# The first batch of a 32-batch attention kernel on Trainium2: where the weight scales are found, how Wo is split and turned, and in which order the first jobs run

## The chip, the cores and the metric

The kernel runs on one core of one Trainium2 chip. Its time is the device time of the whole program in microseconds. Three runs of the kernel before took 1008.40, 1008.94 and 1008.09 us; the median, 1008.4 us, is what the change is measured against.

## The reference

For 32 batches of 256 rows by 512 columns, one layer of graph attention with 16 heads of 32 columns, and a residual. The adjacency matrix is added to the logits (twice, as spatial and as edge encoding).

```python
h = jnp.maximum(_layernorm(x, axis=-1), 0.0)
q = split_heads(h @ Wq.T); k = split_heads(h @ Wk.T); v = split_heads(h @ Wv.T)
a = jnp.einsum('bhnd,bhmd->bhnm', q, k) * D ** (-0.5) + (adj + adj)[:, None]
row_nonzero = jnp.any(a != 0, axis=-1, keepdims=True)
a = jnp.where(row_nonzero, a, -jnp.inf)
p = jax.nn.softmax(a, axis=-1)            # nan -> 0
o = jnp.einsum('bhnm,bhmd->bhnd', p, v).transpose(0, 2, 1, 3).reshape(B, N, D)
x = x + o @ Wo.T
```

x is (32, 256, 512), adj (32, 256, 256) and each weight (512, 512), all in f32.

## The kernel before

**Arithmetic.** Products are made of f16 halves: every operand is split into a rounded part (`_hi`) and the rest (`_lo`), and three products (hi·hi, hi·lo, lo·hi) are summed in PSUM. ScalarE (ACT) writes the rounded part, VectorE (DVE) or GpSimd (POOL) the rest. A weight is brought to a known size first: DVE takes the largest magnitude of each partition (`weight_max`, L610), TensorE (PE) turns the column of 128 maxima into a row (`turn_max`, L881), DVE takes the row's maximum (L616), PE spreads it over the partitions (`spread_max`, L887), and DVE makes the scale by five or more small instructions (`weight_scale`, L622 to L638). PE turns each weight by 16 transposes of 128x128 (`turn_weights`, L873), and ACT and DVE read the turned weight from PSUM and write `w_hi` (L481) and `w_lo` (L650), in four chunks of 128x512.

**Slots.** The program is written out as 34 slots of 16 steps each. Slot number b + 1 works on head 0 to 15 of batch b and prepares batch b + 1: jobs q01, q23, k01, k23, v0, v1 (24 matmuls for a q or k job, 12 for a v job, L978, run in two halves at steps 2j and 2j + 1), and the output jobs o0 and o1 of batch b - 1. In the first slot there are no heads; it makes the weights and batch 0's q, k and v. The second slot has heads but no output jobs. Each engine executes its own list in order, and semaphores tie the lists together. Scores of a group of four heads (L996) are made at steps 12, 0, 4 and 8; `logits` (L690, DVE) follow in the three steps after, then `probs` (L509, exp on ACT with the row sum), the f16 rounding `p` (L522, ACT), the rest of it (L411, POOL), and a transpose by DMA issued from SP (L345). Products with v (`values`, L1046) run at step 12 for heads 0 to 7 and at step 4 of the next slot for heads 8 to 15.

**Around the change.** The first slot has a table of its own (`job_at`, `turn_h_steps`, `v_steps`): jobs 0 to 3 in steps 0 to 7, jobs v0 and v1 in steps 12 to 15, and the second batch's h is turned at steps 9 and 12. The maxima of Wv and Wo are taken at steps 3 and 4 of the first slot on DVE. Wo is turned by PE in the second slot, one chunk of four transposes at each of steps 11 to 14 (`turn_last_weights`, L899), through the two banks that the jobs use (PJ_BANK), and job q01 of the third slot waits until three or four of its chunks have been taken. A store that held a weight is used again later: `pt` for heads 8 to 15 lies in Wq's and Wk's store, `norm_t` in Wv's.

## Time and profile before

| what | us |
|---|---|
| median of three runs | 1008.4 |
| the profiled execution, its own time | 1011.0 |
| its span, first to last instruction | 1009.2 |
| PE busy | 967.0 (96%) |
| ACT busy | 926.8 (92%) |
| DVE busy | 853.0 (85%) |
| POOL busy | 861.7 (85%) |
| first head's exp starts | 48.0 |

The time of the execution is 1.8 us above its span. Shares over the whole span say little of the opening: in the first 48 us no head's softmax runs, and from about 84 us on each slot repeats the one before it. The rows below therefore are of the first 100 us by their starts, with a few of the repeating part to compare.

### The profile page before, as it was taken

What the parts mean: (1) busy time and instruction counts of PE and PEld (TensorE: products, weight loads), DVE (VectorE), ACT (ScalarE), POOL (GpSimd) and SP (SyncE); (2) the same over time, 40 slices, a digit from 0 to 9 for tenths busy, and PEclk for the clock granted to TensorE, in tenths of its full rate; (3) what the DMA queues carried; (4) which work ended last, traced back from release to release, by engine and by line L of the source; (5) the groups of instructions that cost most, each with busy time, mean ns of one, the idle gap of its engine ahead of it and who ended that gap; (6) DMA issues with size and microseconds to landing.
All of it is one profiled execution on the core that took longest, in us unless ns stands there. A gap on an engine that the chain in (4) does not pass through costs nothing.

```text
span 1009.2 us, 33752 instructions
## 1 busy us (share of the span) xinstructions
PE 967.0 (96%) x11596; PEld 666.3 (66%) x11596; DVE 853.0 (85%) x3090; ACT 926.8 (92%) x3025; POOL 861.7 (85%) x936
## 2 busy tenths in 40 slices
PE   6788999999999999999999999999999999999965
PEld 5566766676776667677666777666677766667632
DVE  6778988889898888989888898988889898888863
ACT  3399999999999999999999999999999999999992
POOL 1178989899988989998898999989899988989894
PEclk9899999999999999999999999999999999999988
DMA  6088999999999999999999999999999999999995
GB/s 250 11 145 144 190 188 188 183 193 200 179 190 189 189 188 192 187 199 184 185 182 194 188 201 187 185 194 175 193 192 195 177 196 183 190 188 176 172 178 117
DMA packets 569579, 182.59 MB, mean 181 GB/s; under 512 B 542784, under 2 KB 550976, under 8 KB 569408
## 3 DMA queue, kind: packets, MB, share of 16 engines
q1 hardware_dynamic: 569408, 180.43, 98.1%
q8 instruction: 93, 1.52, 0.6%
q14 instruction: 78, 0.64, 0.2%
HBM read 29.36 MB, written 16.78 MB: 46 GB/s over the span
## 4 chain that ended last, share of the span: by engine, by line
PE 58%; DVE 27%; issue 8%; ACT 5%; POOL 2%; DMA 1%; DVEq 0%; POOLq 0%; ACTq 0%; SPq 0%
PE ps L978 36%; DVE logits L690 14%; PE ps L1046 8%; PE ps L996 7%; DVE stats L595 4%; PE ps L861 3%; ACT probs L509 3%; DVE q_lo L753 2%; DVE o_norm L720 2%; PE ps L1022 1%; DVE some L708 1%; DVE w_max L610 1%; ACT p L522 1%; PE ps L950 1%; POOL p L411 1%
## 5 line engine op out<-in xcount | busy, mean ns | idle before, releaser
L411 POOL TENSOR_TENSOR p<-probs,p 128x512 f16<-128x512 f32 x512 | 586.5, 1162 | 95.8 <-ACT p L522 95.6
L509 ACT ACTIVATE probs<-logits,row_min 128x256 f32<-128x256 f32 x1024 | 514.3, 513 | 1.3 <-DVE row_min L690 1.3
L690 DVE CUSTOM_DVE_ANT_0 logits<-ps,adj_s,sigma 128x256 f32<-128x256 f32 x1024 | 438.0, 475 | 9.8 <-PE ps L996 9.7
L522 ACT ACTIVATE p<-probs 128x512 f16<-128x512 f32 x512 | 324.2, 633 | 0.0
L978 PE MATMUL ps<-ht_hi,w_hi 128*128 128x256 f16 x1024 | 280.9, 274 | 6.4 <-DVE w_lo L650 1.9
L978 PE MATMUL ps<-ht_lo,w_hi 128*128 128x256 f16 x1024 | 280.2, 274 | 0.0
L978 PE MATMUL ps<-ht_hi,w_lo 128*128 128x256 f16 x1024 | 280.1, 274 | 0.0
L509 ACT ACTIVATION_READ_ACCUMULATOR probs<-logits,row_min 128x1 f32 x1024 | 211.4, 206 | 0.0
L978 PEld LDWEIGHTS ps<-ht_hi,w_hi 128*128 128x128 f16 x1024 | 100.4, 98 | 34.3 <-DVE q_lo L753 11.4
L978 PEld LDWEIGHTS ps<-ht_lo,w_hi 128*128 128x128 f16 x1024 | 100.6, 98 | 14.5
L978 PEld LDWEIGHTS ps<-ht_hi,w_lo 128*128 128x128 f16 x1024 | 100.6, 98 | 12.0
L978 PE MATMUL ps<-w_hi,o_hi 128*128 128x512 f16 x248 | 94.7, 382 | 3.6 <-POOL o_lo L437 3.6
L978 PE MATMUL ps<-w_hi,ht_hi 128*128 128x512 f16 x256 | 98.1, 383 | 0.0
L978 PE MATMUL ps<-w_lo,ht_hi 128*128 128x512 f16 x256 | 97.6, 381 | 0.0
L978 PE MATMUL ps<-w_hi,ht_lo 128*128 128x512 f16 x256 | 97.5, 381 | 0.0
L753 DVE SCALAR_TENSOR_TENSOR k_lo<-ps,k_hi 128x512 f16<-128x512 f32 x64 | 43.7, 683 | 63.3 <-ACT k_hi L539 63.3
L978 PE MATMUL ps<-w_hi,o_lo 128*128 128x512 f16 x248 | 94.5, 381 | 0.0
L978 PE MATMUL ps<-w_lo,o_hi 128*128 128x512 f16 x248 | 94.4, 381 | 0.0
L690 DVE DVE_READ_ACCUMULATOR2_ANT row_min<- 128x1 f32 x1024 | 81.4, 80 | 0.0
L422 POOL TENSOR_TENSOR norm<-recip,some 128x256 f32<-128x256 f32 x128 | 78.8, 615 | 1.1 <-PE ps L1022 1.1
L437 POOL TENSOR_TENSOR o_lo<-o_norm,o_hi 128x512 f16<-128x512 f32 x64 | 74.3, 1160 | 5.3
L743 DVE SCALAR_TENSOR_TENSOR v_lo<-ps,v_hi 128x512 f16<-128x512 f32 x64 | 44.2, 691 | 40.3 <-ACT v_hi L549 37.8
(88 smaller groups left out, 1654.9 us busy)
## 6 DMA issues: line engine op xcount, KB each, us to landing
xs<-in_x SPq DMA_DIRECT2D x32, 512.0 KB, 4.5
out<-xs SPq DMA_DIRECT2D x64, 256.0 KB, 2.9
adj_raw<-in_adj SPq DMA_DIRECT2D x32, 256.0 KB, 3.6
pt<-p SPq DMA_TRANSPOSE x256, 4.1
w_nat<-p SPq DMA_TRANSPOSE x256, 3.3
w_nat<-in_L_gnn_Wq SPq DMA_DIRECT2D x1, 1024.0 KB, 6.3
w_nat<-in_L_gnn_Wk SPq DMA_DIRECT2D x1, 1024.0 KB, 9.1
w_nat<-in_L_gnn_Wv SPq DMA_DIRECT2D x1, 1024.0 KB, 11.2
```

What stands on the lines that cost most here:

```text
L411: g.tensor_tensor(p16[:, c % 2, k, 1], probs[:, h % 4].rearrange("p u n -> p (u n)"), p16[:, c % 2, k, 0], ALU.subtract).then_inc(p_split, 1)
L422: g.tensor_tensor(norm[:, c % 2].rearrange("p u (j d) -> p u j d", j=HC), recip[:].unsqueeze(3).broadcast_to(wide), some[:].unsqueeze(3).b ...
L437: g.tensor_tensor(o_lo[:, t.par(d), both, :], o_norm[:], o_hi[:, t.par(d), both, :], ALU.subtract).then_inc(o_split, 1)
L509: e = a.activation(probs[:, h % 4, u, :], logits[:, h % 4, u, :], ACT.Exp, bias=row_min[:, t.par(d), u, h:h + 1], scale=-1.0, accum_out=ro ...
L522: a.activation(p16[:, c % 2, k, 0], probs[:, h % 4].rearrange("p u n -> p (u n)"), ACT.Copy)\
L595: v.bn_stats(stats[:, u, :], xs[:, t.batch(d) % X_RING, u, :]).then_inc(stat_step, 1)
L690: v.tensor_tensor_reduce(out=logits[:, h % 4, u, :], in0=ps[:, S_BANK + h % HC, N * u:N * u + N], in1=adj_s[:, t.par(d), u, :], scale=sigm ...
L743: v.scalar_tensor_tensor(out=v_lo[:, t.par(d), u, :], in0=ps[:, PJ_BANK + u, :], scalar=DOWN, in1=v_hi[:, t.par(d), u, :], op0=ALU.mult, o ...
L753: v.scalar_tensor_tensor(out=lo[:, t.par(1), 2 * g:2 * g + 2, :].rearrange("p c n -> p (c n)"), in0=ps[:, PJ_BANK + g, :], scalar=-DOWN if ...
L978: m = mm(o, l, r, start=start, stop=stop)
L996: m = mm(ps[:, S_BANK + j, N * u:N * u + N], Q[x][HD * j:HD * j + HD, t.par(d), c, P * u:P * u + P], K[y][HD * j:HD * j + HD, t.par(d), c, ...
L1046: m = mm(o, (v_hi, v_lo)[a][:, t.par(d), mh, HD * h:HD * h + HD], pt(c, j)[:, 2 * NU * b + mh:2 * NU * b + mh + NU + 1:NU, :], start=(mh = ...
```

## The change

All edits concern the first two slots, and how Wo lies in SBUF.

1. **Scales from row sums.** For Wk, Wv and Wo, ACT computes the sum of magnitudes of each row of 512 (`sum_weight`, Abs with an accumulated sum, four instructions for a weight), and DVE takes the largest of the four sums of a partition. The scale constants follow (SUM_DOWN, SUM_UP). Wq keeps its true maximum.
2. **Wq in halves.** Its load is two DMAs, and its maximum two DVE instructions of 1024 columns, joined by a third small one.
3. **Second x ahead of Wv** in SP's list of loads.
4. **First slot's order.** Wk is turned and scaled after job q01 instead of before it; the first job of a weight starts chunk by chunk as `w_lo` comes; v0 runs at steps 8 and 9, the first scores at step 12, v1 at steps 13 and 14. Batch 0's second h chunk goes through a bank of its own. The row test of batch 0 moves to the second slot.
5. **Wo.** It is split as it lies (`round_wo` on ACT, `split_wo` on DVE, one row block at each of steps 8 to 11 of the second slot) and turned by four DMA transposes issued from SP at steps 12 to 15; PE's 16 transposes and the wait of job q01 are gone. The output jobs read it as `wo16[:, :, 4*b + c, :]`, four pieces of 128 columns, where they read 512 columns in a row.

```diff
-            load_w(0, wq_d)
+            sp.dma_start(w_nat[:, 0, 0:2], wq_rows[:, 0:2]).then_inc(w_in[0], 16)
+            sp.dma_start(w_nat[:, 0, 2:4], wq_rows[:, 2:4]).then_inc(w_second_half_in, 16)
             load_w(1, wk_d)
+            sp.dma_start(xs[:, 1], xv[1]).then_inc(x_in[1], 16)
             load_w(2, wv_d)
-            sp.dma_start(xs[:, 1], xv[1]).then_inc(x_in[1], 16)
...
-        WO_STEP = 11
+        WO_STEP = 8
+        FIRST_STEPS = [(0, 1), (2, 3), (4, 5), (6, 7), (8, 9), (13, 14)]
...
+                    if t is second and s >= 12:
+                        sp.wait_ge(wo_split, s - 11)
+                        sp.dma_start_transpose(wo16[:, s - 12], w16[:, 2, s - 12]).then_inc(wo16_in, 16)
...
+            def sum_weight(w, o):
+                act.wait_ge(w_in[w], 16)
+                spare = {1: w_nat[:, 0, o, :], 2: probs[:, o].rearrange("p u n -> p (u n)"), 3: w_nat[:, 2, o, :]}[w]
+                a.activation(spare, w_nat[:, w, o, :], ACT.Abs, accum_out=w_sum[:, w - 1, o:o + 1])\
+                 .then_inc(w_summed, 1)
+            def round_wo(o):
+                act.wait_ge(scales_ready, 4)
+                a.activation(w16[:, 2, o, 0:D], w_nat[:, 3, o, :], ACT.Copy, scale=w_scale[:, 3:4])\
+                 .then_inc(wo_hi, 1)
...
-            def weight_max(w):
-                dve.wait_ge(w_in[w], 16)
-                v.tensor_reduce(out=w_max[:, w:w + 1], in_=w_nat[:, w].rearrange("p o k -> p (o k)"),
-                                axis=AX.X, op=ALU.max, apply_absolute_value=True).then_inc(w_max_found, 1)
+            def weight_sum_max(w):
+                dve.wait_ge(w_summed, NC * w)
+                v.reduce_max(w_max[:, w:w + 1], w_sum[:, w - 1, :], AX.X).then_inc(w_max_found, 1)
+            def split_wo(o):
+                dve.wait_ge(wo_hi, o + 1)
+                v.scalar_tensor_tensor(out=w16[:, 2, o, D:2 * D], in0=w_nat[:, 3, o, :], scalar=w_scale[:, 3:4],
+                                       in1=w16[:, 2, o, 0:D], op0=ALU.mult, op1=ALU.subtract).then_inc(wo_split, 1)
...
             turn_weights(0, (0, 1))
             turn_max(0)
-            turn_h(first, 1, 0)
+            turn_h(0, 0)
             spread_max(0)
+            turn_h(0, 1, PJ_BANK + 1)
             turn_weights(0, (2, 3))
-            turn_h(first, 1, 1)
-            turn_max(1)
-            spread_max(1)
-            turn_weights(1)
...
-                                    W[b][:, 3, c, :], i == 0, i == len(steps) - 1))
+                                    wo16[:, :, NC * b + c, :], i == 0, i == len(steps) - 1))
...
-                    if t.batch(1) == 2 and j in (0, 1):
-                        pe.wait_ge(wt_taken, NC * 3 + NC - 1 + j)
+                    if j == 6 and t.batch(-1) == 0:
+                        pe.wait_ge(wo16_in, 16 * NC)
...
+                for i in range(half * part, half * part + half):
+                    o, l, r, start, stop = products[i]
+                    if t.first and j in (0, 2, 4) and i < 12 and i % 3 == 0:
+                        pe.wait_ge(wt_taken, NC * (j // 2) + i // 3 + 1)
                     m = mm(o, l, r, start=start, stop=stop)
```

**ACT, first slot.** Before, from the first rounding of h (`ht_hi`) to the first exp (`probs<-logits`):

```order
L486 ACTIVATE ht_hi<-ps 128x512
L481 ACTIVATE w_hi<-ps,w_scale 128x512 x4
...
L532 ACTIVATE q_hi<-ps 128x512 x2
L539 ACTIVATE k_hi,k_sum<-ps 128x256 x4
...
L486 ACTIVATE ht_hi<-ps 128x512 x2
L549 ACTIVATE v_hi<-ps 128x512
L509 ACTIVATE probs,row_sum<-logits,row_min 128x256 x4
```

In the changed kernel the same stretch (the rows of L514 are the sums of magnitudes, of Wk, Wv and twice half of Wo):

```order
L507 ACTIVATE w_hi<-ps,w_scale 128x512 x4
L514 ACTIVATE w_nat,w_sum<-w_nat 128x512 x4
L570 ACTIVATE q_hi<-ps 128x512
L514 ACTIVATE probs,w_sum<-w_nat 128x512 x4
...
L577 ACTIVATE k_hi,k_sum<-ps 128x256 x2
L514 ACTIVATE w_nat,w_sum<-w_nat 128x512 x2
L587 ACTIVATE v_hi<-ps 128x512
L525 ACTIVATE ht_hi<-ps 128x512
...
L547 ACTIVATE probs,row_sum<-logits,row_min 128x256 x2
```

Twelve sums came in between the roundings, which are spread out: a weight's `w_hi` now stands behind the q or k job that precedes it.

**DVE, first slot.** Before, from Wq's `w_lo` to Wv's scale:

```order
L650 SCALAR_TENSOR_TENSOR w_lo<-ps,w_scale,w_hi 128x512 x4
...
L631 TENSOR_SCALAR sigma<-w_pow 128x1
...
L753 SCALAR_TENSOR_TENSOR q_lo<-ps,q_hi 128x512
L610 TENSOR_REDUCE w_max<-w_nat 128x1 x2
...
L616 TENSOR_REDUCE w_row_max<-ps 1x1
L753 SCALAR_TENSOR_TENSOR k_lo<-ps,k_hi 128x512
...
L690 ISA logits,row_min<-ps,adj_s,sigma 128x256
```

After, from the same `w_lo` to the first logits:

```order
L716 SCALAR_TENSOR_TENSOR w_lo<-ps,w_scale,w_hi 128x512 x4
L649 BN_STATS stats<-xs 128x6 x2
L674 TENSOR_REDUCE w_max<-w_sum 128x1
L815 SCALAR_TENSOR_TENSOR q_lo<-ps,q_hi 128x512
...
L700 TENSOR_SCALAR sigma<-w_pow 128x1
...
L815 SCALAR_TENSOR_TENSOR k_lo<-ps,k_hi 128x512
L724 SCALAR_TENSOR_TENSOR ht_lo<-ps,ht_hi 128x512
L805 SCALAR_TENSOR_TENSOR v_lo<-ps,v_hi 128x512
L752 ISA logits,row_min<-ps,adj_s,sigma 128x256
```

The long reductions over a whole weight are gone from DVE's list after Wq's, and the first logits stand ahead of v1's rest.

**SP, end of the second slot.** Before, the transposes of heads 8 to 15 (into `w_nat`) stand in a row, ahead of the third adjacency load:

```order
L345 DMA_TRANSPOSE w_nat<-p 128x8x128 x8
L355 DMA adj_raw<-in_adj 128x2x256
L345 DMA_TRANSPOSE pt<-p 128x8x128 x6
```

After, Wo's four are put between the last five of them:

```order
L360 DMA_TRANSPOSE w_nat<-p 128x8x128 x4
L369 DMA_TRANSPOSE wo<-w_nat 128x8x128
L360 DMA_TRANSPOSE w_nat<-p 128x8x128
...
L374 DMA adj_raw<-in_adj 128x2x256
L360 DMA_TRANSPOSE pt<-p 128x8x128 x6
```

The middle two rows stand four times in turn; each transpose is of the same size as a head's.

## Rows read from the trace of the kernel before

**Rows 1.** The page's first part: busy time of TensorE over the span

```profile
PE 967.0 (96%) x11596; PEld 666.3 (66%) x11596; DVE 853.0 (85%) x3090; ACT 926.8 (92%) x3025; POOL 861.7 (85%) x936
```

**Rows 2.** Stretches: length; busy us (instructions) per engine; granted clock; DMA share; GB/s

```profile
80.00:84.00 4.00, 3.59 (x36) 2.32 (x36) 3.34 (x12) 4.00 (x13) 3.92 (x5) 0.57 0.37 71
...
150.00:180.00 30.00, 29.88 (x388) 20.81 (x380) 26.36 (x97) 29.11 (x97) 27.38 (x31) 1.00 1.06 193
```

**Rows 3.** Timeline of SP, adjacency loads of two slots 26 apart: start, us

```profile
144.24 0.53 SPq L355 DMA_DIRECT2D adj_raw<-in_adj  x1
...
911.41 0.53 SPq L355 DMA_DIRECT2D adj_raw<-in_adj  x1
```

**Rows 4.** The chain of waits of the first 120 us: start, us, what

```profile
25.43 4.38 DVE w_max L610 x2
...
41.85 2.56 PE ps L978 x6
```

**Rows 5.** Timeline of DVE, first two slots: start, us, instruction, idle before

```profile
7.58 2.29 DVE L610 TENSOR_REDUCE w_max<-w_nat 128x1 f32<-128x2048 f32 x1 [1.00 <-DMA w_nat<-in_L_gnn_Wq]
...
15.91 2.70 DVE L650 SCALAR_TENSOR_TENSOR w_lo<-ps,w_scale,w_hi 128x512 f16<-128x512 f32 x4
...
45.86 0.48 DVE L690 CUSTOM_DVE_ANT_0 logits<-ps,adj_s,sigma 128x256 f32<-128x256 f32 x1 [2.65 <-PE ps L996]
...
80.72 0.48 DVE L690 CUSTOM_DVE_ANT_0 logits<-ps,adj_s,sigma 128x256 f32<-128x256 f32 x1
```

**Rows 6.** Timeline of ACT, first slot and start of the second

```profile
12.48 2.42 ACT L481 ACTIVATE w_hi<-ps,w_scale 128x512 f16<-128x512 f32 x4 [0.69 <-DVE w_scale L638]
...
47.98 0.50 ACT L509 ACTIVATE probs<-logits,row_min 128x256 f32<-128x256 f32 x1
...
53.44 0.62 ACT L522 ACTIVATE p<-probs 128x512 f16<-128x512 f32 x1
53.96 0.58 ACT L532 ACTIVATE q_hi<-ps 128x512 f16<-128x512 f32 x1
```

**Rows 7.** Timeline of PE, first slot

```profile
7.70 1.94 PE L873 MATMUL ps<-ident,w_nat 128*128 128x128 f32 x8 [7.70 <-DMA w_nat<-in_L_gnn_Wq]
...
20.23 0.42 PE L978 MATMUL ps<-ht_hi,w_hi 128*128 128x256 f16 x1
...
22.36 0.29 PE L978 MATMUL ps<-ht_lo,w_hi 128*128 128x256 f16 x1
...
29.04 0.27 PE L978 MATMUL ps<-ht_hi,w_lo 128*128 128x256 f16 x1
30.47 0.28 PE L978 MATMUL ps<-ht_hi,w_hi 128*128 128x256 f16 x1 [1.16 <-DVE q_lo L753]
...
33.61 1.97 PE L873 MATMUL ps<-ident,w_nat 128*128 128x128 f32 x16
```

**Rows 8.** DMA issues of the first 60 us: KB each, median us from issue to landing

```profile
w_nat<-in_L_gnn_Wv SPq DMA_DIRECT2D x1, 1024.0 KB, 11.2
```

**Rows 9.** Timeline of PE, end of the second slot

```profile
75.63 0.66 PE L899 MATMUL ps<-ident,w_nat 128*128 128x128 f32 x4 [1.33 <-DVE v_lo L743]
...
80.41 0.37 PE L978 MATMUL ps<-ht_hi,w_hi 128*128 128x256 f16 x1 [1.91 <-DVE w_lo L650]
...
90.72 0.42 PE L1046 MATMUL ps<-w_nat,v_hi 128*32 128x256 f16 x8
```

**Rows 10.** Timeline of ACT, waits in the second slot's end and the third

```profile
76.32 0.69 ACT L481 ACTIVATE w_hi<-ps,w_scale 128x512 f16<-128x512 f32 x1 [0.63 <-PE ps L899]
...
94.17 0.38 ACT L539 ACTIVATE k_hi<-ps 128x256 f16<-128x256 f32 x1 [0.71 <-PE ps L978]
```

**Rows 11.** The page's costliest groups: an output job's matmul, busy us, mean ns

```profile
L978 PE MATMUL ps<-w_hi,o_hi 128*128 128x512 f16 x248 | 94.7, 382 | 3.6 <-POOL o_lo L437 3.6
```

**Rows 12.** Transposes on SP in 68 to 84 us: ns min/median/max; landing

```profile
L345 SPq DMA_TRANSPOSE w_nat<-p x8: 1232/1312/2222, 68.2 to 82.7; - x8
...
DMA to landing us min/median/max: 3.0/3.2/4.4
```

More of the change, by code:

```diff
@@ L85, in emit @@
         w_nat = sb("w_nat", [P, 4, NC, D])
-        w_hi = sb("w_hi", [P, 4, NC, D], F16)
-        w_lo = sb("w_lo", [P, 4, NC, D], F16)
+        w_hi = sb("w_hi", [P, 3, NC, D], F16)
+        w_lo = sb("w_lo", [P, 3, NC, D], F16)
+        wo16 = sb("wo16", [P, NC, 2 * NC, P], F16)
+        w_half = sb("w_half", [P, 2])
+        w_sum = sb("w_sum", [P, 3, NC])
         w16 = w_nat.bitcast(F16)
@@ L453, in slot @@
                     split_probs(t, s)
+                    if t.first:
+                        continue
                     if s == 3 and later(t, 2):
@@ L557, in slot @@
                 for s in range(H):
-                    if s == 0 and t is second:
-                        take_v(t, 0, 1)
-                    if s in v_steps(t) and t.nxt:
-                        take_v(t, 1, v_steps(t).index(s))
-                    if t.nxt:
+                    if t.nxt and not t.first:
                         if s in (2, 4):
@@ L797, in slot @@
                         take_o(t, 0, 0)
-                    if later(t, 2) and s == 10 and not t.first:
-                        take_h(t, 2, 1, 2 * t.batch(2) + 2)
+                    if s == 10 and not t.first:
+                        for k in h_rests(t, s):
+                            take_h(t.batch(2), k)
                     for b, u in residuals(t, s):
                         residual(b, u)
-                    if s == 1 and t is second:
-                        take_v(t, 0, 1)
-                    if s - 1 in v_steps(t) and t.nxt:
-                        take_v(t, 1, v_steps(t).index(s - 1))
@@ L808, in slot @@
+                    if t is second:
+                        if s == 0:
+                            take_v(t, 0, 1)
+                            weight_row_max(3)
+                        if s == 2:
+                            weight_scale(3)
+                            test_rows(first)
+                        if s - WO_STEP in range(NC):
+                            split_wo(s - WO_STEP)
                     if s % 4 == 3 and t.cur:
@@ L953, in project_last, with project @@
                         m.then_inc(pj_full, full_step(tail, 6 + u))
[L955 to L959 removed]
+            def project(t, j, part):
                 if part == 0:
@@ L1077, in slot @@
                         turn_probs(t, 0, s // 4 - 1)
-                    if later(t, 2) and s in turn_h_steps(t):
-                        turn_h(t, 2, turn_h_steps(t).index(s))
-                    project(t, s)
+                    for k in h_turns(t, s):
+                        turn_h(t.batch(2), k)
+                    for j, half in halves(t, s):
+                        if t.uses(j):
+                            project(t, j, half)
                     if s == 3 and t.prev:
@@ L1091, in slot @@
                         values(t, 0, 0)
-                    if t.nxt and s == 13:
+                    if t.nxt and s == 13 and not t.first:
                         row_test(t)
-                    if t is second and s in range(WO_STEP, WO_STEP + NC):
-                        turn_last_weights(s - WO_STEP)
+                    if t is second and s == 1:
+                        row_test(first)
                     if t is tail and s in (0, 1, 5, 6):
```

268 lines of the change are left out of this document (158 added, 110 removed).

## The prediction

> **What bounds the kernel now.** I read the shares first, then stretches of the repeating part, then the opening as a chain of waits and as a timeline of each engine. Over the span TensorE (PE) is busy 96% of the time [rows 1], and in the repeating part 29.88 of 30 us, ScalarE (ACT) 29.11, VectorE (DVE) 26.36 [rows 2]. A slot there takes (911.41 - 144.24) / 26 = 29.5 us [rows 3]. PE is the bound, ACT has some 0.9 us a slot to spare, and the change takes nothing from a repeating slot. So it can only move the start of that part: each microsecond by which PE's work stands earlier at the third slot comes off the end, as long as nothing behind it is late.
>
> The opening is bound otherwise. The first exp starts at 47.98 [rows 6], behind the first logits at 45.86 [rows 5]. On the way the chain shows DVE with two whole-weight maxima, 4.38 us, with a job's remainder queued behind them, and job v0 near the slot's end, six matmuls of 512 columns in 2.56 us [rows 4], 0.43 each, which is the lower clock. From the first exp to 94 us ACT is nearly full. The third slot's first matmul comes at 80.41, after PE stood 1.91 us for Wo's remainder, and 1.33 us ahead of Wo's second chunk [rows 9]; ACT itself waits 0.63 us for that chunk and 0.71 us for job k01 [rows 10].
>
> **Prices from the rows.** A whole-weight maximum 2.29 us on DVE, half of it 1.15; `w_lo` 2.70 / 4 = 0.675 a chunk [rows 5]. `w_hi` 2.42 / 4 = 0.605; a 128x512 pass from SBUF 0.52 (`p` at 53.44, the next at 53.96); two exps of 256 columns, with their sums, 0.49 apart [rows 6]. A matmul of 256 columns starts every (22.36 - 20.23) / 10 = 0.213 us at first and every (29.04 - 22.36) / 61 = 0.11 us then: 12 take 2.6 or 1.3 us. That is TensorE's level of 1.2 GHz and then the one of 2.4. A 128x128 transpose is 0.22 to 0.24 us at the lower and 0.11 to 0.12 at the higher (8 in 1.94, 16 in 1.97) [rows 7]. Not in the trace is a sum of magnitudes over 512 columns: between 0.52 (without a sum) and 0.98 (two of 256 with one). I take 0.62, near the first, since two instructions are started and two sums read in the 0.98; 12 of them are 7.4 us of ACT, 6.2 to 11.8 at the ends.
>
> **First slot, step by step** (times on the clock of before, us). Wq's second half lands where Wq did, 7.58; the first half's maximum is by then done, so the whole is known at about 9.05 instead of 9.87. PE's list lets 0.5 of that through: eight transposes first (7.70 to 9.64) [rows 7]. Wq's scale comes at 11.9, `w_hi` would start 0.5 earlier but both h chunks now go first: `w_hi` from 12.5 to 14.9, as before [rows 6]. DVE: two h remainders to 13.25, four `w_lo` to 15.95. Job q01 starts with the first chunk at 13.95, not at 20.23: Wk's maximum, scale and turning are no longer ahead of it. It follows the chunks to 16.6 and ends at about 18.4 (17.9 to 19.2 with the clock). ACT sums Wk meanwhile, 14.9 to 17.4. Then Wk is turned (18.4 to 20.6), its scale is ready at 21.9; q23's halves run at 20.7 and 22.3, `w_lo` of Wk comes 23.3 to 25.55 on DVE, k01 runs 24.5 to 27.2, Wv is turned to 29.0, k23 ends at 31.6, v0 at 34.2. Wv landed 11.2 us after an issue in the first 3 us [rows 8], so before 14.2, and lands some 1.4 later behind the second x (512 KB); it is summed from 19.15, so that swap costs nothing. A slower sum (0.98) would delay Wk's maximum by 1.5 us, which q01's second half mostly hides, and Wv's by as much, before it delays k01: about 1 us in all.
>
> After v0: h remainder and v remainder on DVE (35.5 to 36.65), then the first logits at 36.65, against 45.86: 9.2 earlier. The second slot must also take Wo's scale, on DVE between logits (about 1.2 us there), and v1 ends at 39.2. Its q01 waits for the turn of Wo's maximum, which DVE makes behind its logits (40.7), then for nothing: 41.0 to 44.5 with a group of scores inside, the row test to 44.9, then ACT's `q_hi`, which stood at 53.96 [rows 6]. So the second slot runs **9.0** us earlier.
>
> **Second slot's end.** Splitting Wo costs ACT and DVE four passes each, as before; ACT's are 0.52 instead of 0.605 less overlap, 0.2 us in all. Gone are ACT's waits of 0.63 and 0.71 [rows 10] and, I estimate, 0.4 us in ones under 0.2: 9.0 + 0.2 + 1.7 = 10.9 by ACT's list. PE loses 16 transposes and their waits, and starts the third slot when its products with v are done, at some 74.5 of the old clock; but after half a job it must stop for the next batch's first logits, whose last stood at 80.72 to 81.2 [rows 5]. That wait of 5 us is longer than the three before 80.41, after which the matmuls ran at 0.21 apart and the stretch's clock was 0.57 [rows 2, 9]; so I let the lower clock last as long as it did there, about 3.3 us, until 83.7. Before, 80.41 to 85.5 held half a job (12 x 0.213 = 2.6), the scores and the other half (12 x 0.11 = 1.3). After, the first half lies in the wait; the scores begin at 81.2 + 0.3 for the hand-over - 0.8 for the waits that ACT no longer has = 80.7, take 1.3 at the lower clock, and the second half ends at about 84.3: 1.2 sooner. PE: 9.0 + 1.2 = 10.2, less than ACT's 10.9, and from there PE is full as before. **10.2** off; 11.5 if PE stays at the higher clock there.
>
> The four DMA transposes stand in SP's list between those of heads 11 to 15. A transpose holds SP 1.31 us, and lands 3.2 us after its issue [rows 12]. Heads come each 1.5 to 2 us, with a second transpose between two heads SP needs 2.6: the last head's is some 2.7 us late. Products with v need it at 90.72 before [rows 9]; it was issued at 82.7 and landed near 86, a slack of over 4, of which the earlier PE takes 1.2. It just holds: I put 0 in the sum, 2 at the upper end. On a transpose's price the Trainium skill says (DMA: Bandwidth & Descriptors, Latency and other measured facts) that the effective rate is 261 GB/s; for 256 KB that would be an estimate of 1.0 us, so SP's own 1.31 would be what limits, as I have it.
>
> **The sum.** The profiled execution took 1011.0, its span and 1.8 around it. Minus 10.2 it is 1000.8. The median stands 2.6 under that execution, so 1008.4 - 10.2 = **998.2**.
>
> **The rivals.**
> *PE falls to the lower clock at the second slot's head.* In the changed order PE stands 1.5 us between v1 (39.2) and Wo's maximum (40.7), after another 0.75 us. For: after waits of 1.33 and 1.91 us with little between, the 256-column matmuls from 80.41 on took 0.21 each, and the clock granted was 0.57 [rows 2, 9]. Against: a wait of 1.16 us at 29.3 left the pace at 0.11 [rows 7]. Then q01 is 2.6 us longer and the scores 0.6, in front of ACT's `q_hi`: 3 us, of the 10.2 remain 7, time 1001.2. The same price has a first slot that stays at the lower clock until k01 (two halves of 1.3). The Trainium skill (TensorE: Matmul & The Clock Gate, What's actually happening) has it that the throttled state is the default and that activity releases it; by that rule the gaps between chunk-wise matmuls at 14 to 16.6 speak for this rival, and the trace's 10 slow matmuls from 20.23 agree.
> *Wo's transposes are late.* If a transpose takes 2.2 us, the maximum seen [rows 12], the last head's lands 4 x 0.9 = 3.6 us later still, and PE waits about 2 at its values: 1000.2, or 1001 with slower sums.
> *Slower than before: the output jobs read Wo in four pieces.* 24 matmuls a slot in 31 slots, 744 in all, change their moving operand. It decides from 10.2 / 744 = 14 ns each. Against it: products with v read two pieces of 128 columns, and eight of them, four at a time, last 0.42 from start to end at 90.72, no longer than a single whole-row one of 0.27 and one pace of 0.11 more [rows 9, 7]. If four pieces cost 20 ns where two cost none, the time is 998.2 + 14.9 = 1013.
> *The opening's gain does not reach the end* (ACT, DVE or POOL keeps the second slot where it was, or the gain is used up): 1007 to 1010. The small waits of rows 10 and PE's 29.88 of 30 speak against it.
>
> **Chances.** Forecast 0.50 (996.7 to 999.7); clock 0.20 (1000 to 1003); late transposes and slow sums 0.12 (1000 to 1002); more gain than summed, 11.5 or above because PE keeps the higher clock, 0.10 (995 to 997); no gain 0.04; slower 0.04. The range goes from 995.2 to 1002.6. A measurement of this kernel tells 0.2%, 2.0 us, from no change: faster 0.92, same 0.04, slower 0.04.
>
> **What would show it.** Right: first logits at about 36.7, first `p` near 41, q01 from 14 us, in the second slot's end one long wait of PE, for logits, with the third slot's first half job ahead of it, and from the third slot on the same rows as before, 10 us earlier, 29.5 apart. Sums of 0.62 on ACT. Wrong: matmuls 0.21 us apart after 40 us, a wait of values for a transpose in the third slot, or a mean above 382 ns for an output job's matmul [rows 11]. A time above 1004 would mean that a slot's own length changed or that ACT's list in the first slot is the bound.

## The result, and the profile after

The changed kernel took 1005.13 us (median of 5 runs, 1003.96 to 1005.36), the kernel before 1008.94 (5 runs, 1008.09 to 1012.47). The ratio on record is 0.9941 with a 95% interval of 0.9923 to 0.9959, so 5.9 us gained, between 4.1 and 7.8. The two medians alone lie 3.8 us apart: three of the five runs of the kernel before are those behind the prediction's 1008.4, the two others took 1009.77 and 1012.47. A second measurement of both kernels, the first experiment below, gives 5.2 us. Forecast were 998.2 and a gain of 10.2; the time lies 2.5 us above the top of the range. It is faster, by little more than half of what was forecast. That the time lies outside the range is in part a matter of the base: the measured ratio applied to 1008.4 would be 1002.5, just inside. The gain is what missed.

The span of the profiled execution is 1003.4 us, where it was 1009.2. Busy time by the page of the changed kernel, to be read beside [rows 1]:

```profile
PE 959.6 (96%) x11580; PEld 660.2 (66%) x11580; DVE 850.0 (85%) x3092; ACT 934.5 (93%) x3049; POOL 862.3 (86%) x936
```

ACT has 7.7 us more work (twelve sums of 0.61 to 0.65), PE 16 matmuls less, as the change says.

**The repeating part.** The adjacency loads of the changed kernel in SP's timeline, the same two as in [rows 3]:

```profile
138.25 0.53 SPq L374 DMA_DIRECT2D adj_raw<-in_adj  x1
...
905.33 0.53 SPq L374 DMA_DIRECT2D adj_raw<-in_adj  x1
```

They come 5.99 and 6.08 us sooner, and 767.08 apart where it was 767.17. A slot's length is unchanged: all that is gained or missed is decided before 138 us. Twenty-six slots further nothing has been given back.

**First slot.** DVE's timeline of the changed kernel (start, us, instruction, idle before), to be read beside [rows 5]:

```profile
7.86 1.22 DVE L665 TENSOR_REDUCE w_half<-w_nat 128x1 f32<-128x1024 f32 x1 [0.36 <-DMA w_nat<-in_L_gnn_Wq]
...
17.94 0.16 DVE L674 TENSOR_REDUCE w_max<-w_sum 128x1 f32<-128x4 f32 x1 [0.17 <-ACT w_nat L514]
...
37.03 0.48 DVE L752 CUSTOM_DVE_ANT_0 logits<-ps,adj_s,sigma 128x256 f32<-128x256 f32 x1
```

ACT's, beside [rows 6]:

```profile
15.33 0.65 ACT L514 ACTIVATE w_nat<-w_nat 128x512 f32<-128x512 f32 x1
...
41.39 0.62 ACT L560 ACTIVATE p<-probs 128x512 f16<-128x512 f32 x1
...
45.00 0.60 ACT L570 ACTIVATE q_hi<-ps 128x512 f16<-128x512 f32 x1
```

A maximum that took DVE 2.3 us is one of 0.16 over four sums. The first logits come 8.83 us sooner than before (36.65 was forecast, 37.03 came), and `q_hi` of the second slot at 45.00 instead of 53.96: 8.96 us, where the forecast had 9.0. Part of this is the spread between executions: in the six traces of the experiments that leave the first slot as it is here, the first logits stand at 36.14 to 36.66.

**Second slot.** Here the gain is lost. PE's timeline of the changed kernel, its two longest waits between 60 and 85 us:

```profile
67.98 0.40 PE L1063 MATMUL ps<-k_hi,q_hi 32*128 32x256 f16 x4 [3.60 <-DVE row_min L752]
...
76.20 0.29 PE L1063 MATMUL ps<-k_hi,q_hi 32*128 32x256 f16 x4 [1.69 <-DVE row_min L752]
```

These are scores, the first at step 12 of the second slot. The scores' matmuls overwrite a bank that DVE's last logits of the group before must have read, so they wait for `row_min`. The first group is now 4.04 us earlier than before, no longer 8.96. In the kernel before it began here:

```profile
72.02 0.29 PE L996 MATMUL ps<-k_hi,q_hi 32*128 32x256 f16 x4 [0.38 <-DVE row_min L690]
```

DVE's list of the changed kernel just ahead of it (L679 is `split_wo`):

```profile
58.45 1.28 DVE L679 SCALAR_TENSOR_TENSOR w_nat<-w_nat,w_scale 128x512 f16<-128x512 f32 x1 [2.42 <-ACT w_nat L520]
59.66 0.68 DVE L815 SCALAR_TENSOR_TENSOR k_lo<-ps,k_hi 128x512 f16<-128x512 f32 x1
...
61.04 0.75 DVE L679 SCALAR_TENSOR_TENSOR w_nat<-w_nat,w_scale 128x512 f16<-128x512 f32 x1 [0.71 <-ACT w_nat L520]
...
63.64 0.75 DVE L679 SCALAR_TENSOR_TENSOR w_nat<-w_nat,w_scale 128x512 f16<-128x512 f32 x1
...
66.12 0.76 DVE L679 SCALAR_TENSOR_TENSOR w_nat<-w_nat,w_scale 128x512 f16<-128x512 f32 x1
...
67.36 0.47 DVE L752 CUSTOM_DVE_ANT_0 logits<-ps,adj_s,sigma 128x256 f32<-128x256 f32 x1
```

and ACT's (L520 is `round_wo`):

```profile
57.70 0.72 ACT L520 ACTIVATE w_nat<-w_nat,w_scale 128x512 f16<-128x512 f32 x1
...
65.00 0.72 ACT L520 ACTIVATE w_nat<-w_nat,w_scale 128x512 f16<-128x512 f32 x1
```

DVE stands 2.42 and 0.71 us with `split_wo` at the head of its list, waiting for ACT's rounding, while `k_lo` and the logits behind it are queued; all four rests, of 0.75 to 1.28 us, stand ahead of the last logits at 67.36. The 2.42 us are not all new: the kernel before waits at this place too, for `k_hi`:

```profile
66.20 0.69 DVE L753 SCALAR_TENSOR_TENSOR k_lo<-ps,k_hi 128x512 f16<-128x512 f32 x1 [1.89 <-ACT k_hi L539]
```

ACT's four roundings start 0.61 us before what follows them, 2.4 us together, all ahead of the exp of later heads.

Stretches of the changed kernel (length; busy us and instructions of PE, PEld, DVE, ACT, POOL; granted clock; DMA share; GB/s):

```profile
64.00:68.00 4.00, 0.40 (x8) 0.19 (x7) 4.00 (x16) 4.00 (x14) 2.67 (x4) 0.87 0.47 88
68.00:72.00 4.00, 4.00 (x72) 2.80 (x72) 2.34 (x8) 4.00 (x15) 3.16 (x3) 0.50 1.23 145
```

Behind the wait of 3.60 us TensorE ran at 0.50 of 2.4 GHz, the lower of its two levels (1.2 GHz), and the products with v ended at 72.1, so that DVE waited for them:

```profile
72.67 0.69 DVE L782 TENSOR_TENSOR o_norm<-ps,w_nat 128x512 f32<-128x512 f32 x1 [1.87 <-PE ps L1113]
```

From here on the changed kernel catches up 2.05 us, to 6.09 at the adjacency load of the third slot (114.84 before, 108.75 after); PE no longer has Wo's transposes and their waits [rows 9] there, which is the likely reason.

### The profile page after: what moved, and what is told of

Same layout as the page of the kernel before. It is cut to its first block, busy times and chain, and to the rows that moved or that the text cites. A ratio compares the mean times of both kernels' runs of the same rounds, so it can differ in the third digit from the quotient of the medians.

```text
span 1003.4 us, 33752 instructions
## 1 busy us (share of the span) xinstructions
PE 959.6 (96%) x11580; PEld 660.2 (66%) x11580; DVE 850.0 (85%) x3092; ACT 934.5 (93%) x3049; POOL 862.3 (86%) x936
## 4 chain that ended last, share of the span: by engine, by line
PE 56%; DVE 28%; issue 8%; ACT 5%; POOL 1%; DMA 1%; DVEq 0%; POOLq 0%; ACTq 0%; SPq 0%
PE ps L1045 35%; DVE logits L752 15%; PE ps L1113 9%; PE ps L1063 7%; DVE stats L649 4%; ACT probs L547 3%; PE ps L942 3%; DVE q_lo L815 2%; DVE o_norm L782 2%; PE ps L1089 1%; DVE some L770 1%; ACT p L560 1%; PE ps L1019 1%; DMA w_nat<-in_L_gnn_Wq 1%; DVE row_min L752 1%
## 5 line engine op out<-in xcount | busy, mean ns | idle before, releaser
L1045 PE MATMUL ps<-wo,o_hi 128*128 128x512 f16 x496 | 149.2, 383 | 3.8 <-POOL o_lo L456 3.8
L1045 PE MATMUL ps<-wo,o_lo 128*128 128x512 f16 x248 | 94.7, 382 | 0.0
L1063 PE MATMUL ps<-k_hi,q_hi 32*128 32x256 f16 x1024 | 73.1, 276 | 8.2 <-DVE row_min L752 8.2
```

Of the source, the lines that this page charges most:

```text
L1045: m = mm(o, l, r, start=start, stop=stop)
L1063: m = mm(ps[:, S_BANK + j, N * u:N * u + N], Q[x][HD * j:HD * j + HD, t.par(d), c, P * u:P * u + P], K[y][HD * j:HD * j + HD, t.par(d), c, ...
```

## The experiments

Two theories. **Place:** Wo's passes at steps 8 to 11 stand ahead of the last group's logits, and what the first slot gained ends there, with the lower clock as a consequence. **Rival, clock:** the wait would be harmless, the slow matmuls behind it are the loss. Others: the transposes by DMA, or the reading of Wo in four pieces, hold PE; or the first slot's parts were worth less than they seem.

The places of two traces can't be compared by their microseconds alone. With the same first slot, the first logits stand at 36.14 us in one execution and at 37.03 in another, and all that follows shifts with them. So the place of the second slot's step-12 scores is also given from the trace's own first logits on: 26.16 us in the kernel before (72.02 - 45.86), 30.95 in the changed kernel (67.98 - 37.03). That is a loss of 4.8 us.

### The changed kernel again

> The changed kernel itself, timed again beside the others on one chip, as their common yardstick. Both theories expect about 5.9 us less than before (ratio 0.994). Theory D (DVE's list): Wo's split stands ahead of the last group's logits on DVE, waits there for ACT's rounding (2.42 and 0.71 us of idle) and adds 4 x 0.7 us of work, so the scores of the next batch stand at 67.98 where 63 was to be had. Theory A (ACT's list): ACT's four roundings, 4 x 0.61 = 2.4 us, now stand ahead of head 12's exp instead of behind it, and that alone delays the same scores.

1005.39 us (1004.79 to 1006.48), against 1010.6 for the kernel before; ratio 0.9947 [0.9934, 0.9959]. This is the mark for the experiments on the changed kernel; with its spread, less than about 1.5 us can't be told between two of them by time alone. In its trace the scores stand at 67.65, 30.99 us behind the first logits, as in its first trace.

### DVE's rests of Wo behind the logits

```diff
-                        if s - WO_STEP in range(NC):
-                            split_wo(s - WO_STEP)
...
                         logit_rows(t, (s + 3) // 4, *LOGITS[s % 4])
+                    if t is second and s - 1 - WO_STEP in range(NC):
+                        split_wo(s - 1 - WO_STEP)
```

> The changed kernel with one edit: DVE's four passes for Wo's rest stand one step later and behind that step's logits; ACT's list is as in the changed kernel. Theory D: DVE waits no more for ACT's rounding, the last logits of batch 0 come at about 65.0 instead of 67.4, PE waits 1.2 us for them instead of 3.6 and may keep its clock: 2.4 to 4 us less than the changed kernel, 1001 to 1003. Theory A: ACT's list is unchanged, so the time stays within 1 us of the changed kernel, about 1004 to 1005.

1002.23 us (1001.29 to 1002.71), ratio 0.9913 [0.9899, 0.9926]: 3.2 us better than the changed kernel, intervals apart. PE's timeline of this kernel:

```profile
64.16 0.29 PE L1063 MATMUL ps<-k_hi,q_hi 32*128 32x256 f16 x4 [2.24 <-DVE row_min L752]
72.02 0.29 PE L1063 MATMUL ps<-k_hi,q_hi 32*128 32x256 f16 x4 [2.35 <-DVE row_min L752]
```

The scores come 3.82 us sooner as they stand, and 2.97 from the first logits on (27.98, with the first logits at 36.18), with the same four passes done on DVE one step later. Their place is the larger part of the loss. The wait did not shrink to the 1.2 us expected, and the granted clock was 0.57 from 64 to 68 us. DVE's timeline of this kernel shows what stood at the head of its list instead:

```profile
57.00 0.69 DVE L815 SCALAR_TENSOR_TENSOR k_lo<-ps,k_hi 128x512 f16<-128x512 f32 x1 [1.81 <-ACT k_hi L577]
```

DVE waits here too, but for `k_hi`, and `k_lo` starts 2.66 us sooner than the 59.66 of the changed kernel (1.81 from the first logits on).

### PE kept busy through the wait

Twenty-eight matmuls of 256 columns whose result nobody reads, ahead of those scores:

```diff
+                    if t is second and s == 12:
+                        for _ in range(28):
+                            mm(ps[:, PV_BANK, 0:N], w_hi[:, 0, 0, 0:P], w_hi[:, 0, 1, 0:N], start=True, stop=True)
```

> The changed kernel with 28 more matmuls of 256 columns (results not used) ahead of the second slot's step-12 scores, where PE waits 3.60 us at 64.4 us. They last 3.1 us at the higher clock and end before the wait does. Theory C (the clock): after that wait, scores and products with v ran at 0.21 us a matmul (the clock of 68 to 72 us was 0.50) and cost 1.8 us more than at the higher level, and DVE's next step waits for them: time 1.5 to 2 us less than the changed kernel, about 1003. If DVE's or ACT's list alone sets the end, nothing changes (1004 to 1005).

1004.58 us (1003.34 to 1005.21), ratio 0.9936 [0.9924, 0.9948]: 0.8 better than the changed kernel, which the intervals don't tell from nothing; 1.5 to 2 were expected if the clock is the loss. PE and the stretches of this kernel:

```profile
67.54 0.29 PE L1063 MATMUL ps<-k_hi,q_hi 32*128 32x256 f16 x4 [0.56 <-DVE row_min L752]
74.22 0.29 PE L1063 MATMUL ps<-k_hi,q_hi 32*128 32x256 f16 x4 [2.78 <-DVE row_min L752]
```

```profile
68.00:72.00 4.00, 3.44 (x84) 2.62 (x72) 3.47 (x13) 4.00 (x14) 3.22 (x4) 1.00 1.27 151
76.00:80.00 4.00, 4.00 (x27) 3.10 (x25) 3.97 (x21) 2.74 (x9) 2.63 (x4) 0.67 1.19 167
```

The clock stays at 2.4 GHz from 68 to 72 us, and `o_norm` waits 0.53 us instead of 1.87. The scores stand 0.44 us earlier, by as much as this execution already was ahead at 60 us (the job's matmul at 59.92 instead of 60.39). But the next wait, for the next batch's logits, is 2.78 us, and behind it the granted clock is 0.67. That is no effect of the added matmuls alone: between the two traces of the unchanged kernel this wait is 1.69 us once (clock 1.00 from 76 to 80 us) and 2.36 the other time (0.63). What the clock costs is not resolved: 0.8 us by the medians, which may be nothing, and 1.4 at the fourth slot's adjacency load (136.76, against 138.18 in the second trace of the changed kernel; the execution traced was the fastest of its five). The last logits that the scores wait for come no sooner with the higher clock, so the clock is not the cause of the delay at step 12, and at most a part of the whole loss. As the whole cause the rival falls.

### All of Wo in the first slot

The sums of Wo at step 4 of the first slot, its scale at steps 6 to 8, the roundings at 9 and 11, the rests at 9, 14 and 15, the DMA transposes in steps 12 to 15 of the first slot:

```diff
+                        if s == 4:
+                            for o in range(NC):
+                                sum_weight(3, o)
...
                         if s in (9, 11):
-                            sum_weight(3, s - 9)
-                            sum_weight(3, s - 8)
+                            round_wo(s - 9)
+                            round_wo(s - 8)
...
-                    if t is second and s >= 12:
+                    if t.first and s >= 12:
                         sp.wait_ge(wo_split, s - 11)
```

> The changed kernel with all of Wo moved to the first slot: the row sums stand at step 4 on ACT (where it waited 2.74 us for k01), scale, rounding and rest follow at steps 6 to 15, and the four transposes are issued at the first slot's end. No Wo work is left in the second slot on any list. Theories D and A both expect the second slot to lose nothing then: scores of the next batch at about 63.0, the third slot 9 us or more earlier than before; with ACT's 2.4 us gone as well up to 12. Time 996 to 999.5. If the loss had another cause (a second slot that is bound by something else), it stays near 1004.

1000.86 us (1000.27 to 1000.9), ratio 0.9901 [0.9885, 0.9916]: the fastest version with all of the work in it, 9.7 us below the kernel before on its chip (by the ratio 10.0, between 8.5 and 11.6). It is 1.4 us above the range that was expected for it, 996 to 999.5. Its first logits come at 36.35, no later than in the changed kernel, and `q_hi` of the second slot 8.42 us behind them instead of 7.97: the first slot, in which ACT stood idle for 2.74 us before the first k job's `k_hi` (27.75 in the changed kernel's trace), takes Wo's passes for about 0.4 us. PE's timeline:

```profile
63.45 0.29 PE L1067 MATMUL ps<-k_hi,q_hi 32*128 32x256 f16 x4 [0.92 <-DVE row_min L753]
70.18 0.29 PE L1067 MATMUL ps<-k_hi,q_hi 32*128 32x256 f16 x4 [2.83 <-DVE row_min L753]
```

The scores lie 8.57 us ahead of 72.02, of the 9.51 that its first logits are ahead: of the 4.8 us lost, all but 0.9 are back. The fourth slot's adjacency load comes 11.65 us sooner than before (132.59 instead of 144.24), 2.1 more than the first logits' lead, so what PE saves on Wo's transposes arrives too. Why the time gains less than that trace, and less than expected, is open; a wait of 2.83 us for the next batch's logits is left in it, and one of 1.36 at 76.85 for `q_lo`.

### No passes for Wo in the second slot

Wo's roundings and rests are left out, and the four transposes read `w_hi` in their place, so the output lacks the product with Wo:

```diff
-                        sp.wait_ge(wo_split, s - 11)
-                        sp.dma_start_transpose(wo16[:, s - 12], w16[:, 2, s - 12]).then_inc(wo16_in, 16)
+                        sp.dma_start_transpose(wo16[:, s - 12], w_hi[:, 0, 0:2].rearrange("p a k -> p (a k)")).then_inc(wo16_in, 16)
...
-                    if t is second and s - WO_STEP in range(NC):
-                        round_wo(s - WO_STEP)
...
-                        if s - WO_STEP in range(NC):
-                            split_wo(s - WO_STEP)
```

> The changed kernel without Wo's rounding and rest in the second slot: ACT's four and DVE's four passes are left out, the four DMA transposes stay where they were in SP's list and read another store (so the output is not the reference's). Theory: Wo's passes in the second slot are the whole loss, and the transposes on SP cost nothing. Then the time is that of the kernel with Wo in the first slot, 1000.5 to 1001.5 (about 4.5 us under the changed kernel), with the scores of step 12 at 63 to 64 us. Rival: Wo's transposes, between those of heads 11 to 15, make PE wait at its products with v in the third slot; then it is 1 to 3 us slower than that kernel.

1000.65 us (999.86 to 1002.26), ratio 0.9899 [0.9882, 0.9917]: as the version with Wo in the first slot, so moving the passes has brought, within the spread, all that leaving them out can. PE's timeline of this kernel:

```profile
62.90 0.29 PE L1058 MATMUL ps<-k_hi,q_hi 32*128 32x256 f16 x4 [0.92 <-DVE row_min L749]
...
80.73 0.43 PE L1108 MATMUL ps<-w_nat,v_hi 128*32 128x256 f16 x8 [1.41 <-DMA w_nat<-p]
```

The scores are at 62.90, where the forecast needed them (72.02 - 9.0 = 63.0); from the first logits on (36.25) that is 26.65 us, against 26.16 before. The second row is the rival of the late transposes: with PE this early, the products with v wait 1.41 us for a head's transpose, which stood behind Wo's in SP's list. In the changed kernel these products start at 84.74 instead of 78.47, and none waits.

### The new treatment of Wo alone, on the kernel before

The kernel before with `round_wo` and `split_wo` at steps 8 to 11, the DMA transposes and the four-piece reading, and without PE's 16 transposes:

```diff
-        WO_STEP = 11
+        WO_STEP = 8
...
-                    if t is second and s in range(WO_STEP, WO_STEP + NC):
-                        turn_last_weights(s - WO_STEP)
```

> The kernel before, with only the Wo part of the change (split as it lies at steps 8 to 11 of the second slot, turned by DMA, read in four pieces). Theory: the passes at steps 8 to 11 delay the next batch's scores by 2.4 us (ACT) and up to 2.4 (DVE), while the waits of PE for Wo's chunks (1.33, 0.89, 1.91 us) go; the net is near nothing, 0 to 3 us slower than before, so the Wo part took 1 to 5 us from what the first slot gained. Rival (as predicted): the Wo part gains 1.2 us or more by itself.

1012.59 us (12 runs, 1011.39 to 1014.1), against 1010.85 for the kernel before (22 runs): ratio 1.0016 [1.0006, 1.0026], 1.6 us slower. DVE's and PE's timelines of this kernel:

```profile
66.58 1.28 DVE L629 SCALAR_TENSOR_TENSOR w_nat<-w_nat,w_scale 128x512 f16<-128x512 f32 x1 [2.51 <-ACT w_nat L501]
69.18 0.75 DVE L629 SCALAR_TENSOR_TENSOR w_nat<-w_nat,w_scale 128x512 f16<-128x512 f32 x1 [0.72 <-ACT w_nat L501]
```

```profile
76.13 0.29 PE L1012 MATMUL ps<-k_hi,q_hi 32*128 32x256 f16 x4 [3.61 <-DVE row_min L709]
```

The same waits of DVE (2.51 and 0.72) and of PE (3.61) as in the changed kernel, 8 us later, with the old first slot: this part makes the loss by itself. It is a loss where the forecast had a gain of 1.2.

### Which of the passes: ACT's alone, and both behind the softmax work

The changed kernel without DVE's rests, ACT's roundings kept; Wo's transposes read `w_hi` as above, so the output lacks the product with Wo:

```diff
...
-                        if s - WO_STEP in range(NC):
-                            split_wo(s - WO_STEP)
```

> The changed kernel without DVE's four rests of Wo, ACT's four roundings kept where they are; Wo's transposes read w_hi in its place, so the output lacks Wo's product. If DVE's passes ahead of the logits are the whole loss, the scores come at 62.9 as without any pass, and the time is 1000.6. If ACT's 2.4 us ahead of head 12's exp count in themselves, the scores come at 64 to 65.3 and the time is 1002 to 1003.

And with both kept, each behind the softmax work of its step. DVE's rests stand behind the logits as in the second experiment; the new part of the edit is ACT's:

```diff
-                    if t is second and s - WO_STEP in range(NC):
-                        round_wo(s - WO_STEP)
                     exp_rows(t, s + 2)
                     round_probs(t, s + 1)
+                    if t is second and s - WO_STEP in range(NC):
+                        round_wo(s - WO_STEP)
...
```

> The changed kernel with both halves of Wo's split behind the softmax work of their step: DVE's rests one step later behind the logits, and ACT's roundings behind exp and p of their step. If what is left between the version with DVE's rests behind the logits (1002.2) and the one with Wo in the first slot (1000.9) is ACT's roundings ahead of head 12's exp, the time is 1000.9 to 1001.5 and the last group's scores come at 62.9 to 63.5. If it is the eight passes as such (they have to be done somewhere in a full slot), it stays at 1002.0 to 1002.6, with the scores at 64.

ACT's alone: 1002.73 us (1000.5 to 1003.58), ratio 0.9924 [0.991, 0.9937]; both behind: 1002.02 (1001.63 to 1003.34), ratio 0.9917 [0.9904, 0.9931]; the kernel before took 1010.57 beside both. PE, and DVE just before it, with ACT's roundings alone:

```profile
64.34 0.29 PE L1060 MATMUL ps<-k_hi,q_hi 32*128 32x256 f16 x4 [2.13 <-DVE row_min L751]
```

```profile
62.55 0.69 DVE L804 SCALAR_TENSOR_TENSOR v_lo<-ps,v_hi 128x512 f16<-128x512 f32 x1 [0.77 <-ACT v_hi L586]
```

and PE with both behind:

```profile
64.50 0.29 PE L1063 MATMUL ps<-k_hi,q_hi 32*128 32x256 f16 x4 [2.63 <-DVE row_min L752]
```

ACT's roundings cost even with nothing on DVE: what ACT does later (`v_hi`), DVE waits for (`v_lo`), and the logits stand behind that; the scores are 1.44 us later than without any pass, 1.2 from the first logits on (27.86 against 26.65). Moving the roundings behind exp and `p` gains nothing (28.36 from the first logits on, against 27.98 with DVE's rests alone moved): ACT is busy without a gap there (4.00 of 4 us in each stretch from 56 to 72), so the place inside a step does not matter, the 2.4 us do. By the traces the second theory of both expectations holds; the times (1002.0 to 1002.7 against 1000.65) agree, but their intervals overlap, so ACT's part rests on single traces. The profiled execution with ACT's alone was the fastest of its five (1000.5), so its rows tell places better than the time.

### Full maxima on DVE instead of ACT's sums

ACT's twelve sums are left out, and the scale constants follow:

```diff
-                            for o in range(NC):
-                                sum_weight(1, o)
...
-                dve.wait_ge(w_summed, NC * w)
-                v.reduce_max(w_max[:, w:w + 1], w_sum[:, w - 1, :], AX.X).then_inc(w_max_found, 1)
+                dve.wait_ge(w_in[w], 16)
+                v.tensor_reduce(out=w_max[:, w:w + 1], in_=w_nat[:, w].rearrange("p o k -> p (o k)"),
+                                axis=AX.X, op=ALU.max, apply_absolute_value=True).then_inc(w_max_found, 1)
```

> The changed kernel, but the maxima of Wk, Wv and Wo are taken by DVE over the whole weight (2.29 us each) at the places where it took the maximum of four row sums; ACT's twelve sums (0.61 us each) are left out. In the first slot the two maxima of Wk and Wv stand ahead of q_lo and of Wk's rest: k01 about 4 us later, first logits at 40 to 41 instead of 37; Wo's maximum stands among the first logits, 2.3 us more. The sums on ACT then are worth 4 to 6 us: time 1009 to 1011. Rival: DVE had the time, and the order of the first slot is what gained: within 2 us of the changed kernel.

1013.18 us (12 runs, 1011.18 to 1014.08), ratio 1.0019 [1.0009, 1.003]: slower than the kernel before, where 1009 to 1011 was expected. DVE's timeline of this kernel:

```profile
17.18 2.27 DVE L667 TENSOR_REDUCE w_max<-w_nat 128x1 f32<-128x2048 f32 x1
...
40.08 0.48 DVE L746 CUSTOM_DVE_ANT_0 logits<-ps,adj_s,sigma 128x256 f32<-128x256 f32 x1
```

The first logits are 3.05 us later than in the changed kernel, and Wo's maximum, now of 2.27 us, falls among the second slot's logits (PE waits 3.10 us for it at 46.03), so that the second slot's `q_hi` comes at 51.55 instead of 45.00. So Wo's maximum brings 3.5 us on top of the 3.05 at the first logits, where 2.3 was expected. Sums on ACT are worth 1.0019 - 0.9947 = 0.72%, 7.3 us: without them the rest of the change does not pay.

### Wq in one load, the second x behind Wv

```diff
-            sp.dma_start(w_nat[:, 0, 0:2], wq_rows[:, 0:2]).then_inc(w_in[0], 16)
-            sp.dma_start(w_nat[:, 0, 2:4], wq_rows[:, 2:4]).then_inc(w_second_half_in, 16)
+            load_w(0, wq_d)
             load_w(1, wk_d)
-            sp.dma_start(xs[:, 1], xv[1]).then_inc(x_in[1], 16)
             load_w(2, wv_d)
+            sp.dma_start(xs[:, 1], xv[1]).then_inc(x_in[1], 16)
...
```

DVE takes Wq's maximum in one instruction again.

> The changed kernel with Wq loaded and searched as a whole again and the second x behind Wv. Predicted for the halves was 0.5 us at Wq's scale; the order of loads costs nothing as nobody waits for x or Wv. Expected: first logits 0.3 to 0.6 later, time within 1 us above the changed kernel. If the second x held something up, more.

1006.01 us (1004.49 to 1006.49), ratio 0.9946 [0.9931, 0.9961], against 0.9947 for the changed kernel. The first logits stand at 37.10, later than in every trace of the same first slot with the halves (36.14 to 37.03), and 0.4 us later than in the second trace of the changed kernel (36.66), as expected. In time the two edits on the loads are worth nothing that can be measured: 0.6 us between the medians.

## Why the prediction was wrong

**First slot: right.** Four of the marks it named came within 0.4 us: first logits 37.03 (36.65), `p` 41.39 ("near 41"), sums of 0.61 us from start to start (0.62), `q_hi` 45.00 (44.9), so 8.96 for the 9.0. A fifth, the start of job q01, came 0.8 us late (14.75 for 13.95), and the job's end made it good: its last matmul starts at 18.18 (18.4 was forecast). The rival of the lower clock in q01 and at the second slot's head did not come: the second slot's q01 starts at 40.96 with its matmuls 0.11 us apart, and in the first slot the first matmul at 14.75 already ran at the higher pace, 0.11 us from the next, behind PE's f32 transposes, in spite of the wait of 1.35 us and of the gaps between chunks.

```profile
14.75 0.27 PE L1045 MATMUL ps<-ht_hi,w_hi 128*128 128x256 f16 x1 [1.35 <-DVE w_lo L716]
14.86 0.27 PE L1045 MATMUL ps<-ht_lo,w_hi 128*128 128x256 f16 x1
```

The Trainium skill (TensorE: Matmul & The Clock Gate, What's actually happening), which the prediction cited for this rival, has activity release the throttle. The rows agree in so far as PE had made f32 transposes from 7.97 us on (eight in 1.94 us there, eight in 1.06 at 12.33), and show that the gaps between the chunks, on which the rival rested, did not bring the lower level back.

**Second slot's end: the step that failed.** "Splitting Wo costs ACT and DVE four passes each, as before" counted the passes and not their place. Before, they stood at steps 12 to 15, where ACT waited for PE's transposes anyway [rows 10], behind the last logits of the group. The change puts them at steps 8 to 11, ahead of those logits. Queued behind `split_wo` are `k_lo` and the logits, and PE's scores wait for these; the sum had no term for that. The chain is ACT's `round_wo`, DVE's `split_wo`, logits, `row_min`, PE's scores at step 12, and then the lower clock. It takes 4.9 us of the 9.0 by 68 us. The traces side by side (us; "between" is from the first logits to the scores of step 12):

| kernel | first logits | scores | between | PE's wait |
|---|---|---|---|---|
| before | 45.86 | 72.02 | 26.16 | 0.38 |
| changed | 37.03 | 67.98 | 30.95 | 3.60 |
| changed, again | 36.66 | 67.65 | 30.99 | 3.61 |
| PE kept busy | 36.55 | 67.54 | 30.99 | 0.56 |
| before with new Wo | 45.62 | 76.13 | 30.51 | 3.61 |
| DVE's rests behind the logits | 36.18 | 64.16 | 27.98 | 2.24 |
| both behind | 36.14 | 64.50 | 28.36 | 2.63 |
| ACT's roundings alone | 36.48 | 64.34 | 27.86 | 2.13 |
| Wo in the first slot | 36.35 | 63.45 | 27.10 | 0.92 |
| no passes | 36.25 | 62.90 | 26.65 | 0.92 |

By the runs, DVE's place costs 3.2 us of time and 3.0 in this table. ACT's 2.4 us of roundings cost about 1.2 more in the table; in time 1.4 to 2.1 (1002.0 to 1002.7 instead of 1000.65), with overlapping intervals. 0.5 us of the 4.8 is left without an owner. The share of the lower clock in the time is not resolved, 0.8 us by the medians.

**The 1.2 us for PE's transposes, and ACT's 1.9.** Both were reckoned from a third slot that begins as the second slot's products with v allow. What was forecast as one long wait of 5 us there came as two, 3.60 us at step 12 and 1.69 in the next slot. A part of the gain is real: 2.05 us are made good between 68 and 109 us. But with the old first slot this whole part costs 1.6 us instead of bringing 1.2. Only with the passes out of the second slot does the gain reach the forecast's 10.2: it is 10.0 us by the ratio with Wo in the first slot.

**The wait of 5 us and the clock behind it** were thus rightly seen as a thing of this kernel and put in the wrong place. The forecast had the wait at the third slot's first scores, until 81 us of the old clock, which is 72 here, and the lower clock behind it. It came four steps sooner, at step 12 of the second slot: the granted clock was 0.87 from 64 to 68 us and 0.50 from 68 to 72.

**Transposes by DMA: nothing, as put in the sum.** Two of Wo's in SP's timeline of the changed kernel:

```profile
70.50 2.17 SPq L369 DMA_TRANSPOSE wo<-w_nat  x1
...
74.10 1.40 SPq L369 DMA_TRANSPOSE wo<-w_nat  x1
```

They hold SP 1.33 to 2.17 us (1.31 was used), and land 4.4 us after their issue (median). No product with v waited for one. The rival was true in its mechanism and showed only in the version without Wo's passes, as a wait of 1.41 us.

**Four-piece reading of Wo: nothing.** The page's group of an output job's matmul, changed kernel:

```profile
L1045 PE MATMUL ps<-wo,o_hi 128*128 128x512 f16 x496 | 149.2, 383 | 3.8 <-POOL o_lo L456 3.8
```

383 ns where it was 382 [rows 11]; the slower side needed 14 ns more.

**The range** was built around the forecast and the clock; "the gain does not reach the end" had 0.04 and the mechanism "used up", which is what happened to two fifths of it. The sign named for a time above 1004, a slot's own length or ACT's list in the first slot, pointed the wrong way: both were as forecast (767.08 us for 26 slots, first logits at 37.03), and the loss lay between them. A step that moves work ahead of what others wait for deserved a case of its own between 1001 and 1007.

## What to carry to other kernels

When the same passes move to earlier steps, their cost is not their duration but what stands behind them in the list and who waits for it: list the first instruction behind each moved one, and its waiter. Work that has to be done once belongs where its engine waits (here the first slot, in which Wo's passes cost about 0.4 us), not in a stretch where ACT has none to spare and PE waits for what DVE does next. And after an opening has been shortened, look again at every deadline of the next stage, since those that had slack are met first.

## What the runs showed of the hardware

**A small DVE instruction that takes as long as POOL lets it.** DVE's and POOL's timelines of the changed kernel:

```profile
80.83 1.00 DVE L657 TENSOR_SCALAR neg_mean<-mean_var 128x2 f32<-128x2 f32 x1
```

```profile
58.02 1.16 POOL L430 TENSOR_TENSOR p<-probs,p 128x512 f16<-128x512 f32 x1
...
80.66 1.16 POOL L430 TENSOR_TENSOR p<-probs,p 128x512 f16<-128x512 f32 x1 [0.31 <-ACT p L560]
```

An instruction on 128x2 elements takes 1.00 us and ends at 81.83, when POOL's `p` ends (81.82); its neighbour L658 on the same shape takes 0.15. In the other trace of the same kernel the same instruction (at 80.50) falls into a pause of POOL, and takes 0.17. It is not free: `q_lo` stands behind it, and PE waits 1.05 us for that at 82.56. In the other trace that wait is missing; yet the third slot's adjacency load comes no sooner there (108.65 against 108.75), so no price can be given. The first `split_wo` (58.45, 1.28 us; the later ones 0.75) began while POOL's `p` of 58.02 to 59.18 ran. The old rest of Wo had the turned weight in PSUM and one input in SBUF, and was not held. DVE and POOL of the kernel before:

```profile
81.56 0.74 DVE L650 SCALAR_TENSOR_TENSOR w_lo<-ps,w_scale,w_hi 128x512 f16<-128x512 f32 x1
```

```profile
81.52 1.16 POOL L411 TENSOR_TENSOR p<-probs,p 128x512 f16<-128x512 f32 x1
```

It lies wholly beside POOL's and takes its 0.74. The Trainium skill (SBUF — State Buffer, Who interferes with whom) says that a DVE instruction with two SBUF inputs contends with a GpSimd instruction that reads SBUF, one with at most one SBUF input outside the two-port modes does not, that a `tensor_scalar` can enter such a mode, and that whoever comes second is blocked. The rows agree for both splits of Wo; for the 128x2 instruction, which has one SBUF input, the mode is not in the trace. So splitting Wo "as it lies" made its rest able to collide, for 0.5 us at 58.45; the prediction had not weighed that.

**A clock that falls behind one wait and not behind another.** In the changed kernel the granted clock was 0.87 from 64 to 68 us, with 0.40 us of matmuls in these 4 us, and 0.50 from 68 to 72, behind the wait of 3.60. With DVE's rests behind the logits it was 0.57 from 64 to 68, behind a wait of 2.24. A wait of 2.83 us, in two kernels at the same place, had both outcomes. With Wo in the first slot and then without Wo's passes:

```profile
68.00:72.00 4.00, 1.82 (x34) 1.49 (x35) 3.85 (x16) 4.00 (x16) 3.78 (x4) 1.00 1.18 172
```

```profile
68.00:72.00 4.00, 2.37 (x29) 1.48 (x30) 3.85 (x13) 4.00 (x15) 3.92 (x5) 0.67 1.03 183
```

So in these rows the length of a wait alone does not tell whether the clock falls behind it.
